# Scores and value products in two halves each: the first value projection between the halves of the scores, the third key transposes between the halves of the value products

## The reference, cut to what matters

```
q, k, v = split(x @ Wqkv)
q = l2norm(q) * qs ; k = l2norm(k) * ksc      # then rotary tables
sim  = einsum('bhwie,bhwje->bhwij', bq, bk2) * QK_SCALE   # 32 queries by 64 keys per window
sim  = where(mask, -max, sim)
attn = softmax(sim, -1)
out  = einsum('bhwij,bhwje->bhwie', attn, bv2)
x    = out @ Wo + x
```

## Time and profile before

| | |
|---|---|
| median of 3 runs | 3800.83 us (3794.01 to 3806.34) |
| the profiled execution | 3812.88 us, its span 3811.1 us |
| TensorE matmul (PE) | 3382.2 us busy, 89% |
| VectorE (DVE) | 2846.1 us, 75% |
| GpSimd (POOL) | 2380.0 us, 62% |
| ScalarE (ACT) | 2281.7 us, 60% |
| granted clock of TensorE, mean | 0.947 |

### The profile page before, as it was taken

One profiled execution on the slowest core, in us unless ns is written; L12 is line 12 of the kernel. 1 busy time (PEld: TensorE's weight loads), 2 busy tenths in 40 slices (PEclk: granted clock), 3 DMA queues, 4 the chain that ended last, 5 costly groups with the idle time before them and its releaser, 6 DMA issues. The chain is left out here.

```text
span 3811.1 us, 153117 instructions
## 1 busy us (share of the span) xinstructions
PE 3382.2 (89%) x61692; PEld 2170.2 (57%) x61692; DVE 2846.1 (75%) x4178; ACT 2281.7 (60%) x4158; POOL 2380.0 (62%) x2203
## 2 busy tenths in 40 slices
PE   4898998998989999985997789999998998999997
PEld 2665666666666666652222466666665666666664
DVE  3888887888888888863231878888888887888883
ACT  3566665666666666652663566666666666666663
POOL 3767677677677677741000768677677667767762
PEclk7999999999999999997998899999999999999998
DMA  3323323333333323310000332333333323323321
GB/s 99 79 69 98 77 71 94 75 77 91 80 80 88 83 67 81 80 51 3 1 1 29 85 75 68 97 78 83 84 77 84 89 69 88 81 74 83 75 72 37
DMA packets 194546, 273.56 MB, mean 72 GB/s; under 512 B 59788, under 2 KB 85640, under 8 KB 192264
## 3 DMA queue, kind: packets, MB, share of 16 engines
q1 hardware_dynamic: 193800, 263.23, 27.1%
HBM read 35.57 MB, written 1.05 MB: 10 GB/s over the span
## 5 line engine op out<-in xcount | busy, mean ns | idle before, releaser
L1066 POOL TENSOR_TENSOR rot<-t 128x512 f32<-128x512 f32 x768 | 975.7, 1274 | 294.8 <-DVE t L925 280.1
L1072 POOL TENSOR_TENSOR qkn<-rot,rn 128x512 f32<-128x512 f32 x768 | 793.1, 1043 | 167.2 <-DVE rn L948 164.6
L924 DVE TENSOR_TENSOR t<-ps,table 128x512 f32<-128x512 f32 x768 | 526.8, 686 | 246.9 <-ACT sq L731 240.6
L1078 POOL TENSOR_TENSOR prob<-prob,rsum 128x512 f32<-128x512 f32 x192 | 295.6, 1540 | 437.9 <-DVE rsum L967 437.9
L510 PE MATMUL ps<-w_hi,in_hi 128*128 128x512 f16 x1152 | 453.4, 394 | 112.6 <-POOL w_lo L1097 87.1
L925 DVE TENSOR_TENSOR t<-ps,table 128x512 f32<-128x512 f32 x768 | 522.6, 680 | 0.0
L731 ACT ACTIVATE sq<-ps 128x512 f32<-128x512 f32 x768 | 445.2, 601 | 106.3 <-PE ps L512 99.7
L578 PE MATMUL sv_all<-pT,arena 64*64 64x32 f32 x24576 | 414.3, 221 | 65.7 <-issue 65.3
L534 PE MATMUL ps<-ident,qkn 128*128 128x128 f32 x3072 | 457.0, 279 | 10.5 <-issue 7.9
L931 DVE TENSOR_REDUCE n<-sq 128x16 f32<-128x1024 f32 x384 | 464.4, 1209 | 0.0
L737 ACT ACTIVATE arena<-ps 128x512 f32<-128x512 f32 x384 | 227.9, 593 | 385.6 <-PE ps L512 384.5
(11 more groups left out here) (123 smaller groups left out, 5199.5 us busy)
## 6 DMA issues: line engine op xcount, KB each, us to landing
arena<-arena SPq DMA_DIRECT2D x1152, 128.0 KB, 2.4
arena<-arena SPq DMA_DIRECT2D x768, 64.0 KB, 2.0
w_stage<-in_L_ffn_Wqkv SPq DMA_DIRECT2D x12, 1536.0 KB, 7.5
wo_sb<-in_L_ffn_Wo SPq DMA_DIRECT2D x12, 512.0 KB, 4.2
xsh<-xs SPq DMA_DIRECT2D x48, 128.0 KB, 2.6
f_in<-xs SPq DMA_DIRECT2D x48, 128.0 KB, 2.2
xsh<-xs SPq DMA_DIRECT2D x48, 127.8 KB, 3.2
f_in<-xs SPq DMA_DIRECT2D x48, 127.8 KB, 2.4
```

The costliest lines, as they stand in the source:

```text
L924: dve.tensor_tensor(t1[:, b, :].rearrange("p (h d) -> p h d", d=DH), src, cos, ALU.mult)
L1066: pool.tensor_tensor(rot[:, c, :], t1[:, c % 2, :], t2[:, c % 2, :], ALU.add).then_inc(pool_add, 1)
L1072: pool.tensor_tensor(qkn[:, 0, c, :].rearrange("p (h d) -> p h d", d=DH), rot[:, c, :].rearrange("p (h d) -> p h d", d=DH), rn[:, c, :].un ...
```

## The change

`scores` and `outputs` take a part, 0 or 1. Part 0 has the waits (and in `scores` the two mask matmuls) and the first half of the small matmuls, part 1 the second half and the signal. In `step`, `outputs` part 0 stands ahead of `turn_qk(T-1, 2)` and part 1 behind it; `scores` part 0 stands ahead of `values` 0, and part 1 where `scores` was. No instruction is added or removed, and the other engines' programs are the same.

```
-                def scores(T, s):
+                def scores(T, s, part):
 
                     p = s % 2
-                    pe.wait_ge(act_o, tile_done(T - 1, 1, 2))
-                    pe.wait_ge(act_k, tile_done(T, 3, 4))
-                    pe.wait_ge(pool_carry, tile_done(T))
-                    for par in range(2):
-                        pe.matmul(sv[par][:, :], identb[:, :],
...
-                    for pair in range(PAIRS):
+                    if part == 0:
+                        pe.wait_ge(act_o, tile_done(T - 1, 1, 2))
+                        pe.wait_ge(act_k, tile_done(T, 3, 4))
+                        pe.wait_ge(pool_carry, tile_done(T))
+                        for par in range(2):
+                            pe.matmul(sv[par][:, :], identb[:, :],
...
+                    for pair in range(4 * part, 4 * part + 4):
...
-                    last.then_inc(pe_s, 1)
+                    if part == 1:
+                        last.then_inc(pe_s, 1)
...
-                def outputs(T, B, s):
+                def outputs(T, B, s, part):
 
                     v = s % 2
-                    pe.wait_ge(dve_sub, tile_done(T))
-                    pe.wait_ge(act_p, tile_done(T, 1, 2))
-                    wait_apart(pe, v_loaded[s], windows_done(B))
-                    for j in range(4):
+                    if part == 0:
+                        pe.wait_ge(dve_sub, tile_done(T))
+                        pe.wait_ge(act_p, tile_done(T, 1, 2))
+                        wait_apart(pe, v_loaded[s], windows_done(B))
+                    for j in range(2 * part, 2 * part + 2):
...
-                    last.then_inc(pe_pv, 1)
+                    if part == 1:
+                        last.then_inc(pe_pv, 1)
...
                         project(T, q, s, 3)
+                    if two:
+                        outputs(T - 2, B if s >= 2 else B - 1, (s - 2) % TILES, 0)
                     if one:
                         turn_qk(T - 1, 2, two)
                     if two:
-                        outputs(T - 2, B if s >= 2 else B - 1, (s - 2) % TILES)
+                        outputs(T - 2, B if s >= 2 else B - 1, (s - 2) % TILES, 1)
...
                     if s == 3 and f1:
                         f_var(B - 1)
+                    if one:
+                        scores(T - 1, (s - 1) % TILES, 0)
                     if now:
...
                     if s == 1 and f2:
                         f_up(B - 2, 1)
                     if one:
-                        scores(T - 1, (s - 1) % TILES)
+                        scores(T - 1, (s - 1) % TILES, 1)
                     if now:
                         values(T, q, s, 1)
```

More of the change, by code:

```diff
@@ L535, in turn_qk @@
                     last.then_inc(pe_tqk, 1)
-                def scores(T, s):
+                def scores(T, s, part):
                     p = s % 2
-                    pe.wait_ge(act_o, tile_done(T - 1, 1, 2))
-                    pe.wait_ge(act_k, tile_done(T, 3, 4))
-                    pe.wait_ge(pool_carry, tile_done(T))
-                    for par in range(2):
-                        pe.matmul(sv[par][:, :], identb[:, :],
-                                  maskb[:, 1 if s == 0 else 0, :].unsqueeze(1).broadcast_to([P, HPC, KEYS]),
-                                  start=True, stop=False, skip_group_check=True)
-                    for pair in range(PAIRS):
+                    if part == 0:
[4 more added lines that the diff above has]
+                            pe.matmul(sv[par][:, :], identb[:, :],
+                                      maskb[:, 1 if s == 0 else 0, :].unsqueeze(1).broadcast_to([P, HPC, KEYS]),
+                                      start=True, stop=False, skip_group_check=True)
+                    for pair in range(4 * part, 4 * part + 4):
                         for w in range(WPT):
```

## The result

The changed kernel takes 3963.04 us (median, 3954.28 to 3965.05), the kernel before beside it 3802.82 us: a ratio of 1.042, 95% interval 1.040 to 1.044. The forecast was 3928 us, slower, in a range of 3840 to 4000. The profiled execution of the change spans 3963.3 us and that of before 3811.1 us. These two are 152 us apart, and the 152 us are what the views can explain.

What follows compares the result with a forecast made beforehand. TensorE (PE), running nearly without a pause, was taken as the bound. Terms 108 + 36 + 92 - 109 = +127 us gave 3940 against the profiled execution, 3928 us against the median of the runs; range 3840 to 4000.

Steps and rivals of the forecast that it cites:

- The wait for the keys: Before `values` 0: the mask matmul now waits for ScalarE's last copy to `kT`, 0.51 to 0.98 us a step; +108 us.
- The wait for `pT`: Before the third chunk's transposes: value products wait 0.19 us for ScalarE's copies, 192 times; +36 us.
- The changeovers: In scores and value products: one more entrance and exit between whole-array and small matmuls each, 0.48 us, 192 times; +92 us.
- The broken-up runs: Splitting the dense scores and value products shortens PE's "issue" halts, with half of those elsewhere; 46 + 35 + 28 = -109 us.
- The named sign: Sign of being right: "issue" waits in the scores and value products down by half or more.
- a lower clock: Sign of being wrong: a granted clock below that of before, for which the forecast allowed nothing.
- The reading of the halts as ends of instruction packets: In the dense runs, PE uses up a packet of 240 instructions before the next arrives, some 2.9 us per packet.
- Whether fetches are hidden: At 16 KiB block crossings: the skill's rule has fetches mostly hidden, so nothing is gained and the sum is +236, not +127.
- The halts stay: Rival: halts in the dense runs remain although the runs are shorter; +236, 4037 us; chance 0.07.
- Faster: Rival: new pauses in scores and value products replace all halts, changeovers cost nothing; -40, 3761 us; chance 0.06.
- No change: Rival: all halts go and the changeovers cost half; +6, 3807 us; chance 0.05.
- The waits alone: Rival: as forecast in scores and value products, but the changeovers are free; +35, 3836 us; chance 0.04.

Runs made afterwards that it cites:

- scores_relaxed: Kernel before with only the scores split around the first value projection, their first half waiting just for the third copy to `kT`: 3794.41 us (ratio 0.998).
- waits_hoisted: The changed kernel, order untouched, with the waits in the middle of the two split runs taken ahead of the runs: 3998.06 us (1.053 against the kernel before).
- shift_before: Kernel before with 32 small matmuls (128 instructions) added at the start of each stack: 3790.21 us (ratio 0.998).
- around_v1: Kernel before with the scores split around the second value projection instead of the first, value products unsplit: 3849.7 us (ratio 1.012).
- scores_early: Kernel before with the whole scores run ahead of the first value projection, first half waiting only for the third copy to `kT`: 3839.24 us (ratio 1.010).
- scores_only: Kernel before with only the scores split around the first value projection, value products as before: 3895.91 us (ratio 1.026).

## Why the prediction was right

**What bounds it.** PE was taken as running without a pause, so that each new wait is paid in full. The new waits and changeovers (104 + 52 + 93) less what was given back (97) are the 152 us of the two traces. The other engines' work is unchanged. The wait for the keys and the changeovers were sized well. What was given back came out near the forecast partly by luck, as shown below.

**The wait for the keys**, +108: measured +104, and scores_relaxed took 98 us of it away together with 101 us of the time. The 0.10 us from ScalarE's end to PE's start was right for this wait.

**The wait for `pT`**, +36: measured +52. The 0.10 us from ScalarE's end held at s = 1 and s = 3 only. At s = 0 and s = 2 the wait for the value windows comes behind the one for `pT`, as an instruction of its own, and at s = 2 a computation for it too: in the step shown the sequencer's instructions start at 1091.15 (`pT`, L575), 1091.26 (L252) and 1091.36 (L253), and the weight load at 1091.43. The 0.25 us more at s = 2 (48 times) and the 0.04 at s = 0 (46 times) are 14 of the 16 us that were missing. The prediction had set the windows aside because no DMA is waited for there; their wait costs time even when it is over long before. waits_hoisted shows the same effect at the mask.

**The changeovers**, +92: 93, from the usual distances alone. The single prices stayed as they were: the first score comes 0.52 us after the first mask (1096.05 to 1096.57), and a value projection leaves 0.31 us for the second half (1097.81 to 1098.12) where a whole-array matmul would leave 0.21.

**The broken-up runs**, -109: this is the step that was mis-sized. In the dense runs 81 us were expected and 38 came. The named sign, "issue" waits in the two runs down by half or more, didn't come: they went from 129.0 to 100.7 us. Of the other "issue" pauses 28 us were to go and 6 to 11 went. So what was reasoned gave 44 to 49 us of the 109. The rest of the 97, some 50 us, are the shorter wait for weights (22) and the higher granted clock (an estimate of 30), and neither stands in the prediction: it named only a lower clock, as a sign of being wrong. Without these two the traces would lie some 200 us apart. That the forecast of this sum was met within 12 us is luck.

The reading of the halts as ends of instruction packets was right (shift_before), and so was the sign. The sizing assumed that the fetch begins where it began before and gains the whole break; but a large part of the fetches now begin only in the break. In the run shown, the break between the 64th and the 65th matmul is 0.90 us long and the fetch begins 0.14 us into it. It began 0.41 us later in the run than before, so that PE had work for 1.37 us from there, where it had been 0.87: 0.5 us of the 0.9 were gained. And in this run it took 0.38 us longer (at the median over all halts it took as long as before, 2.4 us), so that the halt is shorter by only 0.12 us.

**Whether fetches are hidden.** The Trainium skill's page "Runtime: NRT & Kernel Launch", section "Instruction fetch mechanics", has the crossing of a 16 KiB block mostly hidden. By that nothing would have been given back, and the sum would have been +236. The block size agrees with this case (8.44 MB in 515 packets). By number, most crossings are hidden here too: 112 halts stood in the dense runs of the kernel before for its 515 packets. But those that aren't cost 148 us, and the change took 38 of them away.

**The rivals.** "The halts stay" (4037 us) is refuted in its full form, though half right in the dense runs. "Faster" needed the relief to exceed waits and changeovers; it was 97 against 249. "No change" needed all halts to go, and three quarters of those in the dense runs stayed. "The waits alone" needed free changeovers, and they cost 93 us. That the probabilities would not be delayed held in the change (L566 waits 13.8 us for VectorE, 13.1 before); around_v1 and scores_early show how little slack there was.

## What to carry to other kernels

When work on a saturated engine is reordered, look first at the waits that travel with it: a wait moved ahead of its cover costs that cover, here 104 us, and it may guard data that only a later part reads. Splitting a run of small matmuls costs two changeovers each time, so it pays only where it removes more than that, and here it came out even at best. Where a kernel's pauses sit at fixed distances in the instruction stream, shift the stream once before crediting an edit with what happened to them. And compare the granted clock of the two traces before the rest of a sum is put down to the edit: here it hid an estimated 30 us.

## What was not expected of the hardware

- From the start of a packet on q8 to the end of a halt it was 2.4 to 2.5 us at the median in each of the fourteen traces (2.2 to 2.9 from the 10th to the 90th percentile), while the packet itself took 1.0 to 1.1 us.
- In the broken runs of the value products 64% of the fetches begin in the break, which is 27% of the run's time, and with the waits taken out of it (waits_hoisted) 70%.
- A wait that stands behind the one that ends last costs time though it is over already: with one more instruction of the sequencer the way from the releaser's end to the mask's start rose from 0.10 to 0.25 us at the median, and with two more it is 0.35 us at the value products of s = 2.
- The change was granted the higher clock for more of its time: its four executions have a mean of 0.958 to 0.961, 23 of the kernel before 0.948 to 0.960 (median 0.953). What decides it stays open; scores_only, slower by 2.6%, has 0.946 to 0.953.
